# Causal mask of the differential attention: from eight TensorE products a slot to two in-place VectorE adds

## What is computed

```python
q1, q2 = (q[:, :, 0], q[:, :, 1])          # 16 heads of 64, two attentions
s1 = jnp.einsum('bshd,bthd->bhst', q1, k1) * scale
s2 = jnp.einsum('bshd,bthd->bhst', q2, k2) * scale
s1 = jnp.where(causal, s1, neg_inf)
s2 = jnp.where(causal, s2, neg_inf)
a1 = jax.nn.softmax(s1, axis=-1)
a2 = jax.nn.softmax(s2, axis=-1)
o = jnp.einsum('bhst,bthd->bshd', a1, v1) - lam * jnp.einsum('bhst,bthd->bshd', a2, v2)
return (o.reshape(B, S, h * dh) * (1.0 - LAMBDA_INIT)) @ Wo
```

## Time and profile before

| | |
|---|---|
| median of 3 runs | 1613.26 us (1611.52 to 1615.08) |
| profiled execution | 1610.17 us, span 1608.4 us, granted clock 0.992 |
| TensorE matmul | 1545.9 us busy, 96% |
| TensorE weight load | 1316.6 us, 82% (beside the matmuls) |
| VectorE | 1224.0 us, 76% |
| ScalarE | 915.4 us, 57% |
| GpSimd | 676.8 us, 42% |
| differential attention | from about 392 us to about 1004 us of the span |

### The profile page before, as it was taken

One profiled execution on the slowest core, in us unless ns is written; L12 is line 12 of the kernel. 1 busy time (PEld: TensorE's weight loads), 2 busy tenths in 40 slices (PEclk: granted clock), 3 DMA queues, 4 the chain that ended last, 5 costly groups with the idle time before them and its releaser, 6 DMA issues. The chain is left out here.

```text
span 1608.4 us, 72839 instructions
## 1 busy us (share of the span) xinstructions
PE 1545.9 (96%) x28420; PEld 1316.6 (82%) x28420; DVE 1224.0 (76%) x3513; ACT 915.4 (57%) x2620; POOL 676.8 (42%) x1068
## 2 busy tenths in 40 slices
PE   7999999999999999999999999999999999999795
PEld 5887788787778888888788787799999999999664
DVE  6889888677777777777777776578888888888664
ACT  5777777643545545554554554566666666666251
POOL 3666656511333333333333333234444444444345
PEclk9999999999999999999999999999999999999998
DMA  3214312111131100111110011121212212122231
GB/s 102 72 46 114 80 54 57 48 54 46 51 73 31 29 26 26 28 27 28 31 29 26 26 30 29 42 60 48 64 48 59 62 44 64 48 59 60 82 114 35
DMA packets 157669, 82.55 MB, mean 51 GB/s; under 512 B 17641, under 2 KB 153115, under 8 KB 157568
## 3 DMA queue, kind: packets, MB, share of 16 engines
q1 hardware_dynamic: 154800, 77.68, 18.0%
q0 software_dynamic: 2048, 3.15, 0.6%
q10 hardware_dynamic: 720, 0.33, 0.1%
HBM read 61.03 MB, written 21.27 MB: 51 GB/s over the span
## 5 line engine op out<-in xcount | busy, mean ns | idle before, releaser
L1493 PE MATMUL bank<-diff_xT,diff_w_score 128*32 128x128 f32 x8192 | 249.1, 273 | 1.7 <-DVE diff_z L1723 0.9
L1493 PEld LDWEIGHTS bank<-diff_xT,diff_w_score 128*32 128x32 f32 x8192 | 219.2, 110 | 25.0 <-issue 19.2
L1618 ACT ACTIVATE diff_keys<-bank 128x512 f32<-128x512 f32 x256 | 152.3, 595 | 148.6 <-PE bank L1493 148.4
L2097 ACT ACTIVATE lat_prob<-bank,lat_neg_max 128x128 f32<-128x128 f32 x512 | 181.1, 367 | 94.5 <-DVE lat_neg_max L2252 93.7
L1808 POOL TENSOR_TENSOR diff_prob<-diff_prob,diff_inv_sum 128x512 f32<-128x512 f32 x64 | 67.0, 1047 | 337.9 <-DVE diff_inv_sum L1711 337.9
L2314 POOL TENSOR_TENSOR lat_prob<-lat_prob,lat_inv_sum 128x512 f32<-128x512 f32 x128 | 133.4, 1042 | 146.3 <-DVE lat_inv_sum L2234 145.4
L2020 PE MATMUL bank<-lat_catT,lat_query 128*128 128x128 f32 x1024 | 139.2, 279 | 2.3 <-ACT lat_query L2108 2.1
L1988 PE MATMUL bank<-lat_catT,lat_w_score 128*128 128x128 f32 x1024 | 137.9, 278 | 3.1 <-issue 2.5
L2008 PE MATMUL bank<-lat_w_vo,lat_ctxT 128*128 128x128 f32 x1024 | 130.3, 275 | 1.1 <-ACT lat_ctxT L2120 1.1
L1988 PEld LDWEIGHTS bank<-lat_catT,lat_w_score 128*128 128x128 f32 x1024 | 124.4, 192 | 4.8 <-issue 3.8
L2020 PEld LDWEIGHTS bank<-lat_catT,lat_query 128*128 128x128 f32 x1024 | 124.4, 192 | 4.7 <-ACT lat_query L2108 3.7
(11 more groups left out here) (274 smaller groups left out, 3688.4 us busy)
## 6 DMA issues: line engine op xcount, KB each, us to landing
lat_c_rep<-cat SPq DMA_DIRECT2D x128, 128.0 KB
stage<-low_y SPq DMA_DIRECT2D x64, 64.0 KB, 1.6
diff_x_rep<-stage SPq DMA_DIRECT2D x128, 32.0 KB, 1.7
lat_c_t<-cat SPq DMA_DIRECT2D x32, 128.0 KB, 2.2
exp_w<-in_L_ffn_w_dram SPq DMA_DIRECT2D x16, 256.0 KB, 3.0
expert_rows<-latw_zeros SPq DMA_DIRECT2D x4, 548.0 KB, 6.5
exp_rows<-expert_rows SPq DMA_DIRECT2D x8, 274.0 KB, 3.6
low_x_t<-in_x_dram SPq DMA_DIRECT2D x32, 64.0 KB, 1.9
```

Of the source, the lines that this page charges most:

```text
L1493: last = nc.tensor.matmul(ring[(k + d) % 2][at, j * P:(j + 1) * P], w_score[:, H1 * (k // 2) + HS * d + 4 * (k % 2) + j, at], xT[:, :], st ...
L1618: nc.scalar.activation(keys[:, k // 2, 4 * (k % 2):4 * (k % 2) + 4, :].rearrange("p h t -> p (h t)"), ring[(k + d) % 2][:, :], ACT.Copy).t ...
L2097: last = nc.scalar.activation(prob[:, q, m, :], ps_s[q][:, m * T:(m + 1) * T], ACT.Exp, bias=neg_max[:, q, m:m + 1], accum_out=row_sum[:, ...
```

## The change

VectorE adds the triangle in place to the scores in their banks, and the eight mask products of a slot are gone. `scores(n)` now issues four products for the high scores, raises `s_done`, issues four for the low ones and raises it again. `shift` begins with two adds, the high one after the first `s_done` and the low one after the second, each raising the new semaphore `masked`; the high maximum waits for the first of them, the low maximum for the second. `tri` becomes f32. The wait for `tri_done` moves from TensorE to VectorE.

```diff
-        tri = sb("tri", [P, L], BF16)
+        tri = sb("tri", [P, L])
...
-        tri_done = sem("tri_done")
+        tri_done, masked = sem("tri_done"), sem("masked")
...
                 for q in range(4):
                     b, qi = q // 2, q % 2
-                    nc.tensor.matmul(ps_hi[L * q:L * (q + 1), :].rearrange("p (h t) -> p h t", h=HS),
-                                     xT[:, b * S + L:(b + 1) * S], keys[:, 1 - qi, :, b * S:(b + 1) * S],
-                                     start=True, stop=False)
+                    last = nc.tensor.matmul(ps_hi[L * q:L * (q + 1), :].rearrange("p (h t) -> p h t", h=HS),
+                                            xT[:, b * S + L:(b + 1) * S], keys[:, 1 - qi, :, b * S:(b + 1) * S],
+                                            start=True, stop=True)
+                last.then_inc(s_done, 1)
                 for q in range(4):
                     b, qi = q // 2, q % 2
-                    nc.tensor.matmul(ps_lo[L * q:L * (q + 1), 0:LO].rearrange("p (h t) -> p h t", h=HS),
-                                     xT[:, b * S:b * S + L], keys[:, qi, :, b * S:b * S + L],
-                                     start=True, stop=False)
-                mask = tri[:, None, :].to_broadcast([P, HS, L])
-                for at in strips:
-                    last = nc.tensor.matmul(ps_hi[at, :].rearrange("p (h t) -> p h t", h=HS)[:, :, L:S], core.identb[:, at],
-                                            mask, start=False, stop=True)
-                last.then_inc(s_done, 1)
-                for at in strips:
-                    last = nc.tensor.matmul(ps_lo[at, 0:LO].rearrange("p (h t) -> p h t", h=HS), core.identb[:, at], mask,
-                                            start=False, stop=True)
+                    last = nc.tensor.matmul(ps_lo[L * q:L * (q + 1), 0:LO].rearrange("p (h t) -> p h t", h=HS),
+                                            xT[:, b * S:b * S + L], keys[:, qi, :, b * S:b * S + L],
+                                            start=True, stop=True)
                 last.then_inc(s_done, 1)
...
-                            pe.wait_ge(tri_done, 4)
...
+                above = tri[:, None, :].to_broadcast([P, HS, L])
                 dve.wait_ge(s_done, 2 * n + 1)
+                nc.vector.tensor_tensor(hi[:, :, L:S], hi[:, :, L:S], above, ALU.add).then_inc(masked, 1)
+                dve.wait_ge(s_done, 2 * n + 2)
+                nc.vector.tensor_tensor(lo, lo, above, ALU.add).then_inc(masked, 1)
+                dve.wait_ge(masked, 2 * n + 1)
                 nc.vector.tensor_reduce(row_max[:, d, 1, :], hi, AX.X, ALU.max).then_inc(max_done, 1)
...
-                dve.wait_ge(s_done, 2 * n + 2)
+                dve.wait_ge(masked, 2 * n + 2)
                 nc.vector.tensor_reduce(row_max[:, d, 0, :], lo, AX.X, ALU.max).then_inc(max_done, 1)
...
+            dve.wait_ge(tri_done, 4)
             pairs(dve, pair, lambda i: latent.vector(dve, i))
```

## The result

The changed kernel takes 1635.85 us in the median of 4 runs (1634.67 to 1636.99), against 1612.39 (1611.24 to 1615.08) of the kernel before. The ratio is 1.0143, with a 95% interval of 1.0127 to 1.0159: 20 to 26 us slower, by the medians 23.5. The forecast was 1637.6, 24.3 us slower. The profiled execution took 1634.67 us with a span of 1633.0 and a granted clock of 0.992, the clock of before. The span grew by 24.6 us.

What follows compares the result with a forecast made beforehand. TensorE was taken to bound the kernel at 18.74 us a pair, VectorE's chain with the adds afterwards at 19.48. 22.9 + 0.8 + 0.5 gives 24.3 us on 1613.26: 1637.6 us, range 1624 to 1654.

Steps and rivals of the forecast that it cites:

- What bounds the kernel: In differential attention, TensorE's own work sets the pair of batches (two slots, d=0 and d=1) at 18.74 us, without steady-state waits.
- VectorE's chain: VectorE's dependent steps over a pair, from z to the next z, sum to 18.08 us, 0.66 shorter than TensorE's.
- The removed products: Eight mask products a slot take 0.22 us of TensorE's stream, 0.44 a pair, 14.1 us in all at most.
- The adds: Two in-place mask adds a slot on VectorE cost 0.35 us each, 1.40 a pair.
- the bounds 0.27 and 0.47: Limits in us on one VectorE add: extra cost of 512 elements over 256, and an add whose reader follows directly.
- The wait for the low scores: On VectorE, now ahead of the high maximum; the scores are there no later than masked high ones were, so costs nothing.
- The loop through z: In d=0 TensorE's second key bank waits for z on VectorE, behind the lengthened shift; pair 19.48 us, 0.74 longer.
- The sum: Over the phase, 31 pairs give 22.9 us, one-time instruction L1269 0.8, adds behind the last z wait 0.5: 24.3.
- TensorE's waits: Some 30 for z and as many for the mix copies, together some 38 us: 24 lost, 14 of removed work.
- rival E: TensorE's clock falls with its new idle time; at the lower level a fifth of the time, the 590 us phase grows by a fifth; chance 0.02.
- Rival B: VectorE's idle quarter takes the adds and TensorE keeps its 14.1 us: 1599.2 us, faster; chance 0.06.
- Rival C: Only the d=1 slot stalls, VectorE recovering in d=0; TensorE gives back its 0.44 a pair: 1613 us; chance 0.04.

Runs made afterwards that it cites:

- e5: The changed kernel with the causal mask left out, neither mask products nor adds: 1602.96 us against 1610.72 for the kernel before, pair 18.30.
- e8: The changed kernel with each add right in front of the maximum that needs it: 1653.60 us, ratio 1.0264 to the kernel before.
- e7: The changed kernel with the high add alone, the low scores' mask left out: 1622.73 us, ratio 1.0081 to the kernel before.
- e2: The changed kernel with z right behind the high maximum (d=0) and mix copies ahead of the high sums (d=1): 1605.14 us, ratio 0.9939.
- e6: The kernel before, mask products kept, plus two in-place adds of zeros a slot on VectorE: 1640.51 us, ratio 1.0191.
- e1: The changed kernel with z moved on VectorE, in d=0, right behind the high maximum: 1615.47 us, ratio 1.0000 to the kernel before.
- e4: The changed kernel with only the mix copies moved ahead of the high sums in d=1: 1638.97 us, ratio 1.0161 to the kernel before.
- e10: As e2, but in the pair behind the last one z stands behind the shift again: 1604.05 us, ratio 0.9938 to the kernel before.
- e9: The changed kernel with the low add alone, ahead of the high maximum, the high scores' mask left out: 1615.24 us, ratio 1.0001.
- e3: The kernel before, mask products kept, with z early and the d=1 mix copies ahead of the high sums: 1613.28 us, ratio 0.9996.

## Why the prediction was right, point by point

**What bounds the kernel.** TensorE before, at 18.74 a pair; VectorE's chain 0.66 behind it. e5 shows the chain at or under 18.30. The changed kernel's 19.39 less four steps of 0.335 is 18.05, and with the steps of 0.46 and 0.47 this chain gives 19.89 for e8 (measured 19.93) and 18.99 for e7 (19.00). The 18.08 of the prediction was 0.03 too long, a matter of rounding over ten steps.

**The removed products** are worth 0.22 a slot (e5, e2). In the changed kernel next to none of it is realized, as forecast: e6, which keeps them, is 0.07 a pair longer and not 0.44. The prediction calls one product 0.29 long; that row covers four of them, and a single one is 0.27. Its sum doesn't use this.

**The adds** cost 0.33 or 0.34 each, forecast 0.35, between the bounds 0.27 and 0.47; the upper bound is real in another order (e7, e8). The wait for the low scores, put at nothing, cost nothing: the low add starts 0.33 behind the high one with no idle time (601.74, 602.07). The prediction took from the Trainium skill, "VectorE: DVE Perf Modes", section "The DRAIN you can't avoid", that the next operation doesn't start until the pipeline is empty, which would put every add at about its length of 0.43; the runs show 0.33 to 0.34 where nothing depends and 0.46 to 0.47 where the next one does. That was half of the section: it goes on that a next operation that is not held starts earlier. By the section "Two Vector instructions with no wait between them" of the same page, only a held instruction waits until every earlier one has finished. The steps of 0.33 behind adds of 0.43 agree with that.

**The loop through z.** The 0.34 from z to the second key bank and the 2.65 from there to the mix copies were read from a pair that a one-time instruction had delayed. In the changed kernel they are 0.34 and 607.58 - 604.93 = 2.65, in every pair within 0.01. e1, which relieves this link alone and takes the loss away, and e4, which relieves the other and doesn't, show that it is this one.

**The sum.** 31 x 0.74 = 22.9 was forecast for the pairs, 0.8 for L1269 and 0.5 behind the last wait. The trace gives its 24.6 in parts: the first z is 1.7 later than before; the two pairs with L1269 are 20.51 instead of 19.32, 1.2 each; 26 pairs are 0.65 longer, 16.9; one pair, at the entry of the loop, is 1.7 longer, of which 0.65 is the loop through z. Up to the 30th z that is 22.8, and 1.8 more come behind it. 24.6 against 24.3: that they lie so close is in part luck, since errors cancel in it. The pairs were put 0.09 too long, 2 to 3 us, and the delay at the entry of the loop, about 1 us, and the 1.8 instead of 0.5 behind the 30th z were not foreseen. The median came out 1.8 us under the forecast of 1637.6, and half of that is the kernel before, whose median was 0.9 lower with the fourth run. TensorE's waits, forecast at some 38 us, read 23.3 as idle time of its products; the 38 is right only when counted by starts (24.6 lost and 14.1 of removed work).

**The clock** stayed at 1.00 in the stretch with the stalls, so rival E didn't come up there. It did come up once in e4, behind a wait of 1.93 us, and the pair that holds it is 1.5 us longer than in the changed kernel. The prediction's 2 in 100 was for such a fall in every pair; none of the runs shows that. **Rival B**, the idle quarter of VectorE that takes the adds, came true only in e2 and e10, once the order let it, and with 9.7 and 10.7 us of its 14.1. **Rival C** had the right second link, the mix copies, at the wrong time: it is the limit of e1.

## What to carry to other kernels

An engine that is busy three quarters of the time can still be a few per cent from setting the pace. Add up its chain from one value that the full engine waits for to the next, start to start, and compare that sum with the full engine's period; the difference is what new work may cost. And where work has moved to an engine, look at what stands behind it in that engine's order and is awaited elsewhere: here two moves of short instructions turned 1.4% slower into 0.6% faster. The in-place adds here, 0.43 us long, cost their engine 0.33 where something unrelated stood behind them and 0.46 where their reader did.

## What the runs showed of the hardware

Not expected: in every kernel without the mask products TensorE stands still once, in the first pass of the hardware loop, for something that the profile calls issue. In the changed kernel:

```profile
475.62 1.26 PE L1493 MATMUL bank<-diff_xT,diff_w_score 128*32 128x128 f32 x36
478.01 1.07 PE L1493 MATMUL bank<-diff_xT,diff_w_score 128*32 128x128 f32 x28 [1.14 <-issue]
```

1.14 us here, 1.7 in e4, e5 and e9, one time in a run. In the kernel before, in e3 and in e6, whose TensorE program has the eight products a slot, no such wait is longer than 0.3 in the loop. So in these twelve kernels it goes with TensorE's instruction stream and not with VectorE's order: e2 and e3 have the same two moves, and only e2 has the wait. DMA traffic rises just before (208 GB/s from 470 to 475 us), but it does so in e6 as well (214 GB/s), without the wait. What TensorE waits for wasn't tried.
